# Moving GpSimd's chunks and gathers, and the top layers' small steps, to other steps of the round

## The reference

```python
x0 = xk = e                       # (1024, 32, 16)
for W in (W0, W1, W2):            # 32 x 32 x 64, then 32 x 64 x 64 twice
    xk = relu(einsum('bmd,bhd,mhk->bkd', x0, xk, W))
    outs.append(sum(xk, axis=2))  # (1024, 64)
z = concatenate(outs, axis=1)
h = concatenate([z, dense_ctx], axis=1)
h = maximum(h @ W_top1 + b_top1, 0)   # 208 -> 512
h = maximum(h @ W_top2 + b_top2, 0)   # 512 -> 256
y = h @ W_top3                        # 256 -> 1
```

## The kernel before

| step | (stream, layer) | chunks | of them on GpSimd |
|---|---|---|---|
| 0 | (2t, 0) | 4 and the squares | 0 |
| 1 | (2t-1, 2) | 16 | 2 |
| 2 | (2t, 1) | 16 | 4 |
| 3 | (2t+1, 0) | 4 and the squares | 0 |
| 4 | (2t, 2) | 16 | 4 |
| 5 | (2t+1, 1) | 16 | 2 |

## Time and profile before

### The profile page before, as it was taken

How to read it: one execution, slowest core, us unless ns; L and a number is a source line. 1 busy time by engine, 2 the same in 40 slices (tenths; PEclk the granted TensorE clock), 3 DMA queues, 4 the chain that set the end, 5 groups by cost and what they waited for, 6 DMA issues and landing times.

```text
span 697.3 us, 7219 instructions
## 1 busy us (share of the span) xinstructions
PE 581.6 (83%) x2752; PEld 199.7 (29%) x2752; DVE 569.7 (82%) x295; ACT 231.7 (33%) x425; POOL 453.7 (65%) x348
## 2 busy tenths in 40 slices
PE   0040788999899989999899979998999989999978
PEld 0010222223332323323332324232332333233424
DVE  0020899998899998898889898898889889999963
ACT  0100361433325162615224242616243331616031
POOL 6776016188966978487948888487948896636120
PEclk9995799999999999999999999999999999999989
DMA  5498639059591949368672949195855949193000
GB/s 152 153 392 313 259 136 351 1 174 363 174 360 36 379 151 378 127 213 324 249 285 90 398 129 394 63 329 206 310 224 158 377 148 386 24 384 124 1 0 0
DMA packets 54244, 151.95 MB, mean 218 GB/s; under 512 B 9697, under 2 KB 18913, under 8 KB 54210
## 3 DMA queue, kind: packets, MB, share of 16 engines
q1 hardware_dynamic: 46018, 149.39, 57.1%
q0 software_dynamic: 8192, 2.11, 2.4%
HBM read 147.26 MB, written 4.20 MB: 217 GB/s over the span
## 4 chain that ended last, share of the span: by engine, by line
POOL 43%; issue 29%; PE 17%; DVE 3%; ACT 3%; POOLq 2%; SPq 1%; DMA 1%; DVEq 0%
POOL emb L281 25%; POOL zg L293 18%; PE acc L474 15%; DVE zd L360 3%; POOLq L292 2%; ACT xk_sb L389 1%; ACT xk_ps L389 1%; DMA z2d_y<-dense_t_in 1%; PE mlp L515 1%; ACT relu_ab L396 0%; PE mlp L506 0%; PE mlp L507 0%; PE acc L482 0%; DVE zpart L340 0%; PE mlp L562 0%
## 5 line engine op out<-in xcount | busy, mean ns | idle before, releaser
L360 DVE TENSOR_TENSOR zd<-rolled,xk_ps 128x2048 f32<-128x2048 f32 x244 | 543.9, 2282 | 112.5 <-issue 41.8
L474 PE MATMUL acc<-zd,w_sb 128*64 128x512 f32 x1696 | 401.0, 605 | 60.1 <-issue 33.5
L293 POOL TENSOR_TENSOR zg<-rolled,xk_sb 128x1024 f32<-128x1024 f32 x88 | 208.9, 2379 | 152.9 <-ACT xk_sb L389 151.8
L281 POOL DMA_INDIRECT emb<-tables_in,index x256 | 244.5, 955 | 69.2 <-issue 64.6
L474 PEld LDWEIGHTS acc<-zd,w_sb 128*64 128x64 f32 x1696 | 116.3, 138 | 317.7 <-issue 218.9
L389 ACT ACTIVATE xk_ps<-acc 64x512 f32<-64x512 f32 x128 | 73.0, 570 | 104.9 <-issue 52.9
L474 PE MATMUL acc<-zg,w_sb 128*64 128x512 f32 x352 | 91.4, 597 | 14.9 <-POOL zg L293 14.4
L474 PE MATMUL acc<-zd,w 128*64 128x512 f32 x256 | 63.0, 612 | 37.4 <-issue 36.7
L389 ACT ACTIVATE xk_sb<-acc 64x512 f32<-64x512 f32 x128 | 75.7, 591 | 3.1
L396 ACT ACTIVATE relu_ab<-acc 128x512 f32<-128x512 f32 x48 | 28.7, 597 | 122.7 <-issue 72.1
L474 PEld LDWEIGHTS acc<-zg,w_sb 128*64 128x64 f32 x352 | 23.8, 136 | 70.7 <-POOL zg L293 35.6
(11 more groups left out here) (46 smaller groups left out, 69.9 us busy)
## 6 DMA issues: line engine op xcount, KB each, us to landing
rolled<-x_scratch SPq DMA_DIRECT2D x256, 512.0 KB
base<-x_scratch SPq DMA_DIRECT2D x16, 512.0 KB
emb<-tables_in,index POOLq DMA_INDIRECT x256
x_scratch<-emb SPq DMA_DIRECT2D x32, 128.0 KB
w_sb<-w_in SPq DMA_DIRECT2D x2, 512.0 KB
wt<-wtop_in SPq DMA_DIRECT2D x1, 512.0 KB
wt1a<-wtop_in SPq DMA_DIRECT2D x1, 256.0 KB
w<-w0a_in SPq DMA_DIRECT2D x1, 160.0 KB
```

The lines of the kernel that those rows point to most:

```text
L281: pool.indirect_dma_start(emb[:, i % 2, c * DIM:(c + 1) * DIM], None, tables, bass.IndirectOffsetOnAxis(index[:, g:g + 1].bitcast(U32), 0) ...
L293: nc.gpsimd.tensor_tensor(zg[:, n % ZG_BUFS, :], rolled[:, s, j, :], xk_sb[:, s, :], ALU.mult).then_inc(zg_ready, 1)
L360: nc.vector.tensor_tensor(zd[:, n % ZD_BUFS, 0:w, :], rolled[:, s, j:j + w, :], repeated(xk_ps[:, s, :], w), ALU.mult).then_inc(zd_ready, 1)
L474: end = nc.tensor.matmul(acc[h * MAPS:(h + 1) * MAPS, s, :], weights, z[:, h * HALF:(h + 1) * HALF], start=(i == 0 and c == 0), stop=(i == ...
```

## The change

In numbers: GpSimd has four chunks in steps 2 and 5 and two in steps 1 and 4, in place of four in steps 2 and 4 and two in steps 1 and 5. The phase (1, 1) of the head also gets four in place of two. The five gathers before step 0 are gone, and the numbers after the chunks are new: 2 in step 1, 11 in step 2, 2 in step 4, 17 in step 5. `zsum` comes after step 2's last chunk on TensorE, and ScalarE copies its result after the evacuation of step 2. `mlp2` moves from two thirds of step 5 to just behind its first item, and `mlp3` from behind step 5 to two thirds of it; ScalarE takes y before the evacuation of step 5.

```diff
-POOL_CHUNKS = {(0, 0): 0, (1, 0): 0, (0, 1): 4, (1, 1): 2, (0, 2): 4, (1, 2): 2}
-POOL_CHUNKS_FIRST = {(0, 0): 0, (1, 0): 0, (0, 1): 0, (1, 1): 2, (0, 2): 0, (1, 2): 2}
+POOL_CHUNKS = {(0, 0): 0, (1, 0): 0, (0, 1): 4, (1, 1): 4, (0, 2): 2, (1, 2): 2}
+POOL_CHUNKS_FIRST = {(0, 0): 0, (1, 0): 0, (0, 1): 0, (1, 1): 4, (0, 2): 0, (1, 2): 2}
...
-GATHERS_FIRST = 51
-GATHERS_BEFORE = 5
-GATHERS_AFTER = {1: [4, 5], 2: [1, 1, 1, 5], 4: [3, 1, 1, 1], 5: [2, 2]}
+GATHERS_FIRST = 50
+GATHERS_AFTER = {1: [1, 1], 2: [1, 1, 1, 8], 4: [1, 1], 5: [1, 1, 1, 14]}
...
-                if q < len(ORDER) - 1:
-                    if k == 2:
-                        zsum_to_sb(m)
-                    if k == 4:
-                        h1_to_sb(m)
-                    if k == 5:
-                        h2_to_sb(m)
+                if k == 4:
+                    h1_to_sb(m)
+                if k == 5:
+                    h2_to_sb(m)
+                    y_to_sb(m)
                 evacuate(q)
-                if k == 5:
-                    y_to_sb(m)
+                if k == 2:
+                    zsum_to_sb(m)
...
-                    if between is not None and i == len(merged) * 2 // 3:
-                        between()
+                    if "early" in between and i == 0:
+                        between["early"]()
+                    if "late" in between and i == len(merged) * 2 // 3:
+                        between["late"]()
...
-                phase(q + 2, lambda: zsum(m))
+                phase(q + 2)
+                zsum(m)
                 phase(q + 3)
-                phase(q + 4, lambda: mlp1(m))
-                phase(q + 5, lambda: mlp2(m))
-                mlp3(m)
+                phase(q + 4, late=lambda: mlp1(m))
+                phase(q + 5, early=lambda: mlp2(m), late=lambda: mlp3(m))
```

More of the change, by code:

```diff
@@ L308, in _ @@
                 k = (q - HEAD) % 6
-                if q >= HEAD and k == 0:
-                    gathers(GATHERS_BEFORE)
                 if PLAN.pool[q]:
@@ L458, in _, with phase @@
         def _(pe):
-            def phase(q, between=None):
+            def phase(q, **between):
                 stream, layer = ORDER[q]
@@ L539, in _ @@
                 phase(q + 1)
-                phase(q + 2, lambda: zsum(m))
+                phase(q + 2)
+                zsum(m)
                 phase(q + 3)
-                phase(q + 4, lambda: mlp1(m))
-                phase(q + 5, lambda: mlp2(m))
-                mlp3(m)
-            phase(len(ORDER) - 1, last_sums)
+                phase(q + 4, late=lambda: mlp1(m))
+                phase(q + 5, early=lambda: mlp2(m), late=lambda: mlp3(m))
+            phase(len(ORDER) - 1, late=last_sums)
             m = TILES - 1
```

## The result

| | us |
|---|---|
| before, median of 4 runs | 698.72 (697.3 to 700.25) |
| changed, median of 4 runs | 730.58 (729.39 to 731.48) |
| ratio | 1.0456 [1.0441, 1.0472] |
| profiled execution of the changed kernel, its span | 730.73, 728.8 |

What follows compares the result with a forecast made beforehand. TensorE's waits for GpSimd chunks delayed by gathers were taken to bound the kernel. Steps 1 to 4 gain 5.5, steps 4 to 1 8.6, head +1.2, tail -1.2: 699.1 - 14.1 = 685.0 us, range 678 to 692.

Steps and rivals of the forecast that it cites:

- What hides the fourteen gathers: Behind step 5: GpSimd ends the gathers at 364.2, its first chunk of step 1 can't start before 365.4, slack 1.2 us.
- The walk of step 5: TensorE runs step 5 without a wait, 15.96 us plus 0.53 for `mlp3`; the evacuation starts at 360.55 instead of 361.99.
- step 4 to 1: VectorE's passage from step 4 to the next step 1: 38.84 us in place of 40.28, a gain of 1.44 a round.
- (e): Rival, chance 0.07: the fourteen gathers hold GpSimd into step 1, TensorE waits for its first chunk; 712 us at 2.0 each.
- round: One whole round on VectorE: 74.60 us in place of 76.86, from gains of 1.44 and 0.82.
- step 1 to 4: VectorE's passage from step 1 to step 4, 36.58 us before, forecast to gain 0.82 us.
- VectorE's wait before step 1: Wait for the evacuation ahead of step 1, up from 1.39 to about 2.7 us, since the evacuation then bounds it.
- last round, step 4 to its last phase: Without gathers to lose in step 4, 37.49 us becomes 38.84 less 0.1: 1.2 us lost.
- the whole: Sum over the kernel: 5.5 from steps 1 to 4, 8.6 from steps 4 to 1, head +1.2, tail -1.2; 14.1 us gained.
- The wait of 2.81 us in step 5: VectorE's wait for a free buffer because TensorE is behind; forecast to be gone, the buffer being free at 337.5.
- The gain of 0.82 from step 1 to 4: In step 2, 0.82 us a round from `zsum` moved behind the phase and GpSimd's last chunk made some 8 us early.
- The 0.53 for `mlp3`: `mlp3` moves ahead of step 5's evacuation, adding 0.53 us to step 5 and cutting the gain of 1.97 to 1.44.

## Why the prediction was wrong

**The step that failed** is "What hides the fourteen gathers". It priced them as GpSimd's time alone, 17.5 us with a slack of 1.2, and put what they do to the other engines at nothing, without a reason. The price holds: the row was over at 296.99 + 1.25, and GpSimd idled 7.80 us behind it. The walk of step 5 beside it ("run by TensorE without a wait", "the evacuation starts at 360.55") took TensorE's signals as immediate. On the chip where before and after were first measured they are not, beside a long row: the evacuation waited 6.3 us for one that was due, and step 4 to 1 took 45.33 us, not 38.84. The runs that show it are the row taken apart (45.33 to 39.13 us with nothing else changed), the new gathers on the old chunks (the wait is there), and the same kernel on the other kind of chip (no signal late, 39.06 us).

**The trace of before had it.** I read the earlier trace rows for VectorE and ScalarE at 122 to 134, and the earlier trace rows for the pitch of a gather, and did not look at what ScalarE did beside the first row of 51. Three rows of before, of ScalarE, TensorE and GpSimd:

```profile
68.50 2.35 ACT L389 ACTIVATE xk_ps<-acc 64x512 f32<-64x512 f32 x4 [35.99 <-issue]
```

```profile
41.89 2.15 PE L474 MATMUL acc<-zd,w 128*64 128x512 f32 x8
```

```profile
65.63 0.94 POOL L281 DMA_INDIRECT emb<-tables_in,index  x1 [0.30 <-issue]
```

TensorE ends the first phase at 44.04, ScalarE evacuates it at 68.50, 24.5 us later and 2.9 after the last gather starts. That is about the whole difference of 25 us between the kinds of chips (a round of before is the same on both: 76.86 here, 263.29 - 186.42 = 76.87 with the cut head on the faster chip), and it foretold this result: fourteen gathers in a row end some 18 us after they begin, and what TensorE signals in the second half of them waits for the end. A smaller case stood in the very round that I walked, beside seven gathers in a row:

```profile
360.60 0.62 ACT L412 ACTIVATE h<-mlp,bt 128x128 f32<-128x128 f32 x2 [11.76 <-remote]
```

`mlp2` had ended at 358.36 (the matmuls of `mlp2` start at 356.31 and take 2.05), 2.2 us before `h2_to_sb` starts; in the last round, without gathers, it starts 0.04 us after `mlp2` ends.

**The rivals.** (e) had the right culprit and side, and the wrong mechanism: it wanted a pitch of 1.85 us and more, and the pitch stayed at 1.25. Its 712 us fell 19 short of what was measured. The Trainium skill, "DMA: Bandwidth & Descriptors", section "Anatomy of one DMA — SWDGE (gpsimd) path", gives a fixed cost of about 2.0 us. As time of the engine the rows deny it again: the fourteen gathers start 1.25 us apart.

**Each term, where no signal is held.** The forecast's own clock can be read on the faster chip, against the kernel before there:

| term | forecast | measured there |
|---|---|---|
| round | 74.60 | 256.47 - 181.63 = 74.84 |
| step 1 to 4 | 35.76 | 217.41 - 181.63 = 35.78 |
| step 4 to 1 | 38.84 | 39.06 |
| VectorE's wait before step 1 | about 2.7 | 2.67 |
| last round, step 4 to its last phase | 38.7 | 630.67 - 591.61 = 39.06 |
| the whole | -14.1 | 661.1 - 673.77 = -12.7 |

The walk was right within 0.2 us a passage (0.3 in the last round), and 0.2 us in six rounds is most of the 1.4 us by which the sum was too large. The wait of 2.81 us in step 5 is gone, as forecast (0.34 and 0.91 are left, for the reads of `zd`). GpSimd reached `xk_sb` 1.60 us early, where 1.2 was forecast. The gain of 0.82 from step 1 to 4 was booked for `zsum` and GpSimd's last chunk together, and only together it comes: with the old gathers the moved `zsum` alone gained nothing (36.64 us), since TensorE then waited 0.64 us for that chunk. The 0.53 for `mlp3` was not measured by itself.

**Where the time is lost, closed.** On the slower chip the round shown is 81.84 us, on the faster 74.84. Of the 7.0, 6.27 lie in steps 4 and 5 and 0.73 in steps 1 to 4. The lower clock of TensorE behind its idle time adds nothing that can be seen in this kernel: the 6.27 are already the 6.3 of the late signal. The whole spans differ by 728.8 - 658.4 = 70.4 us: 32.75 up to the first step 1 (139.54 against 106.79; the first evacuation alone starts at 70.78 in place of 43.24), 37.2 in six rounds (the last of them with a row of eleven only), 0.4 behind.

**What stays open.** Why TensorE's signals are held beside gathers, and why in four sets of runs and not in two, no run tells. No chip of the later five sets came twice, so that it is the chip and not its condition at the time is not shown either. In all seventeen traces every recorded signal of VectorE, ScalarE and GpSimd comes within 0.02 us of the end of its instruction; only TensorE's are late. But the traces with late signals also lack some records (of TensorE's 370 signals 333 at most are there, of VectorE's 294 at most 242, of GpSimd's none is missing), and those without late signals lack at most two. Whether the two belong together is not known. What ends a hold is bounded only: chunks of 2.4 us after at most five gathers avoid nearly all of its cost, one-column writes do nothing, a wait of some microseconds in the middle of fourteen leaves no cost in step 5.

## What to carry to other kernels

Where a wait is named after an unknown or remote releaser, look for the instruction that should have released it and compare its end with the start of the waiter; a gap of microseconds is a late signal, not late work, and the engine that did the work is innocent. Before making a row of one kind of instruction longer, find the longest such row in the trace and read what every other engine does beside it, not only how long the row takes. Of the plans run on both kinds of chips, the one that gains on both spreads the gathers in rows of at most five among the chunks and cuts the first row: 666.6 us where the kernel before takes 698.7, and 662.0 where it takes 673.4. On the second kind it is no faster than the changed kernel (661.1).

## What the runs showed of the hardware

- On some chips the semaphore signals of finished matmuls are held while GpSimd issues indirect DMAs at a pitch of 1.25 us: 0.5 us late after some eight microseconds of a row, up to 2.6 in a row of eight, up to 11.0 in a row of fourteen, 24.5 in a row of 51. In a row of fourteen the held ones come together, 3.7 us after the start of its last gather. On others, in the same program, they are 0.02 us behind the matmul.
- Only TensorE's signals are held. In the same rows those of VectorE and ScalarE come 0.01 us after the instruction's end.
- The medians of the kernel before are 698.5 to 698.9 us on the one kind and 673.4 to 673.8 on the other. A comparison holds only for the kind it was made on: 1.0456 on one, 0.9817 on the other, for the same pair.
- Cutting the long first row makes the kernel before 21 us shorter on the one kind and 0 on the other, so most of what separates the chips for this kernel is the signal of its first phase.
- TensorE's granted clock can fall behind an idle time of 2 to 3 us and need not: a mean of 0.76 over seven microseconds in three of seven passages of one trace, which are 0.8 us longer each, and 1.00 in the others.
